# Graph network on one core: edge sums earlier, and the tail's first loads beside the drain

## The chip, the cores and the metric

The kernel runs on one core of one Trainium2 chip, written out by hand for each engine: TensorE (PE), VectorE (DVE), ScalarE (ACT), GpSimd (POOL) and SyncE (SP). The metric is the device time of one execution in microseconds; the median of several runs is quoted, and the profile is of one execution of its own.

## The reference, cut to what matters

```python
h = relu(layernorm(x))                            # 6250 nodes, 256 features
q = (h @ Wq + bq) * 32 ** -0.5;  k = h @ Wk + bk;  v = h @ Wv + bv
s = sum over each head's 32 features of q[src] * k[dst]     # 100000 edges, 8 heads
p = exp(s - max of s over the edges of one src)
att = segment_sum(p / segment_sum(p) * v[dst], src)
x = x + att @ Wo + bo
h = relu(layernorm(x))
aggr = segment_sum(edge_attr, dst)                # 100000 x 256, sorted by dst
u = relu(concat([h, aggr]) @ W1 + b1)
x = x + relu(u @ W2 + b2) @ W3 + b3
```

All of it is float32.

## The kernel before

**Stages.** The edges are first sorted by src on DVE while PE, ACT and SP project q, k and v for 49 tiles of 128 nodes. Then come the *batches*: 214 of them, numbered 2 to 215 (`VB` = 2, `NBT` = 216), each of 512 sorted edge slots. Four batches are a *group* (`SG` = 4). Last comes the *tail*: for each of 49 tiles of nodes the output projection, the layernorm and the three layers of the perceptron.

**One batch.** POOL gathers 512 rows of k and v with four indirect loads (`gather`, L791) into a ring of ten buffers in `U` (`NKG` = 10). PE spreads the query rows over the slots (`group_expand`, L1438). DVE multiplies them with k (L2202), reduces (L2209), once a group runs the chain of segment maxima (`group_chain`, L2217 to L2250), and weights v (`group_weighted`, L2256 and L2258). ACT takes the exponentials. PE adds the weighted rows up per node (`group_weighted`, four matmul calls a batch, eight records at L1452); ACT copies a finished group out (L1088), and SP writes it to `g_log` (L635).

**Order.** Each engine has a function `grouped_rounds`, a loop over rounds `b` from 2 to a few past 215. In round b DVE scores batch b and weights batch b - 5 (`LG` = 5), PE spreads batch b + 2 and adds up batch b - 6, POOL runs ahead as far as free buffers and PE's spreads let it. Extra work is hung on round numbers. After the last round DVE sets `T_ZC`, ACT raises `act_over`, SP waits until every row of `g_log` is written and raises `sp_over`.

**Edge sums.** `aggr` is made beside all this: 98 chunks of 1024 edges, eight *sums* each, a sum being 128 edges against a one-hot matrix (`agg_sum`, L1266, two records). The one-hots are ACT's (L947, L949), ACT issues the loads of 512 KB (L507), SP writes the chunks to `ag_dram`. `agg_by_batch` says how many sums are through after round b: 112 before round 2, all 784 after round 191. From `AE` = 192 hang the steps that need them all: `far_rows` (round 196), masks (195, 199, 203), places, the table of rows `rowi` (209), and the *border sums*: POOL loads one row per chunk after its last gather (`border_sums`), DVE adds `F2` in round 217 (`G2_AT`), POOL stores them back.

**Start of the tail.** SP then loads the sums of tiles 0 to 8 into `pa` (`load_sums`, L666), PE makes the two biases' rows (L1210), turns `pa` with 18 transposes (`turn_sums`, L1564), which ACT copies to `aT` (L1134), and multiplies them by half of W1 into banks that are kept (`sums_by_w1`, L1571). ACT copies the biases to `brep` (L1141). SP loads x per tile (`ld`, L701), POOL the rows of `g_log` by `rowi` (`tiles_in`, L807); six tiles have buffers (`NL` = 6). All these buffers lie in `U`, over the ring. DVE adds the biases to six tiles (`bias_rows`, L2370), then goes tile by tile: `norm_rows` (L2360), `x1_stats` (L2383), and so on. PE's tail loop is `turn_h2` (L1588), `turn_rows` (L1596), `wo_mm` (L1612), then the perceptron (L1629 to L1650).

```python
            with e.Else():
                grouped_rounds()
                e.wait_ge(act_over, 1)
                e.wait_ge(tv.s, T_ZC)
...
            e.wait_ge(s_pa, 16)
            for g, half in ((1, 0), (1, 1), (2, 0), (2, 1), (0, 0)):
                turn_sums(g, half)
```

Of the kernel before, what the change touches and what calls it, by code (L numbers as in the profile page):

```python
# [12 lines left out]
P = 128  # L13
# [40 lines left out]
def gnn_kernel(nc, x, src, dst, ea, Wq, bq, Wk, bk, Wv, bv, Wo, bo, W1, b1, W2, b2, W3, b3, out):  # L54
# [30 lines left out]
    with ExitStack() as st:  # L85
# [171 lines left out]
        MTo = [VG.take(P) for _ in range(2)]  # L257
        fG = base[:, 0:NGR]
# [73 lines left out]
        pa = EBO[:, 0:NPT * D].rearrange("p (t d) -> p t d", d=D)  # L332
        ot = [W.take(RW) for _ in range(NL)]
        xt = [W.take(D) for _ in range(NL)]
        at = [W.take(D) for _ in range(NL)]
# [3 lines left out]
        aT = [W.take(2, 512) for _ in range(3)]  # L339
# [10 lines left out]
        brep = W.take(2, D)  # L350
# [46 lines left out]
        row_mm = sem("row_mm")  # L397
# [30 lines left out]
        def agg_by_batch(b):  # L428

            chunks = NCH - C0  # L430
            m = 0
            while (m + 1) * AE // chunks <= b:
                m += 1
            at, rounds = m * AE // chunks, (m + 1) * AE // chunks - m * AE // chunks
            return AGG0 + 8 * m + -(-8 * (b - at + 1) // rounds) if m < chunks else AGG_STEPS
# [43 lines left out]
        AE = NBT - SG - 20  # L479
# [6 lines left out]
        TURNED = {1: (3, 5), 2: (6, 7), 0: (3,)}  # L486
# [36 lines left out]
        def sync_program(e):  # L523
# [150 lines left out]
            with e.If(more_):  # L674
# [10 lines left out]
                e.sem_inc(sp_over, 1)  # L685
            with e.Else():
                grouped_rounds()
                e.sem_inc(sp_over, 1)
                load_sums()

            def ld(w):
                if w >= NT:
                    return
                i, n = w % NL, rows(w)
                if w == 0:
# [3 lines left out]
                if w >= NL:  # L699
                    e.wait_ge(w_x1, w - NL + 1)  # L700
# [7 lines left out]
            for w in range(3):  # L708
                ld(w)
# [12 lines left out]
        def pool_program(e):  # L722
# [93 lines left out]
            def border_sums():  # L816
                e.wait_ge(row_mm, 3)
                e.wait_ge(all_done, 1)
                assert pl.on(e.memset(G2, 0.0)) == G2Z
                e.wait_ge(pl.s, G2Z)  # L820
                rows_in(G2, ag_dram, NP, ixi[:, 2:3]).then_inc(s_g2, 16)

            def border_sums_back():
                e.wait_ge(tv.s, T_G2)
                rows_out(ag_dram, NP, ixi[:, 2:3], G2).then_inc(s_g2, 16)

            def tiles_in(log, n):
                for w in range(NT):
# [5 lines left out]
            with e.If(more_):  # L834
                for b in range(VB + len(early), NBT):
                    gather(b, NKV)
                border_sums()
# [3 lines left out]
                border_sums_back()  # L841
# [12 lines left out]
                tiles_in(o_log, NB * P)  # L854
# [1614 lines left out]
```

## Time and profile before

| | |
|---|---|
| median of 3 runs | 1730.67 us (1730.32 to 1735.76) |
| the profiled execution's own time | 1730.11 us |
| its span, first to last instruction | 1728.3 us |
| busy share of the span | DVE 88%, PE 86%, POOL 55%, ACT 51% |
| batches | 362 to 1458 us |
| tail | 1458 to 1728 us |

Times inside the span count from its first instruction. A group's time is read between two starts of L2202, four batches apart. PE's records of one matmul overlap, as their ends are modelled; its pace is read from start to start.

### The profile page before, as it was taken

How to read it: one execution, taken by the hardware profiler on the slowest of the kernel's cores; microseconds unless marked ns; L12 is line 12 of the kernel's file. 1: busy time of each engine (PE TensorE's matmuls, PEld its weight loads, DVE VectorE, ACT ScalarE, POOL GpSimd, SP SyncE). 2: the span in 40 equal slices, each digit the busy share in tenths (PEclk: the TensorE clock that was granted, in tenths of full speed). 3: DMA queues.
4: the chain of work that ended last, by engine and by line, in shares of the span. 5: the costliest groups of instructions: out<-in, count | busy, mean ns of one | idle time of the engine just before them, and what ended most of it. 6: DMA issues, size and time to landing. Idle time of an engine off the chain costs nothing.

```text
span 1728.3 us, 25001 instructions
## 1 busy us (share of the span) xinstructions
PE 1486.6 (86%) x6926; PEld 1073.2 (62%) x6926; DVE 1523.7 (88%) x2994; ACT 881.0 (51%) x2624; POOL 950.1 (55%) x1002
## 2 busy tenths in 40 slices
PE   4699998868988899888898888888988765899998
PEld 4545556646766667667766676666766544666664
DVE  9998897879999999999999999999999995766663
ACT  4744445746556556666656555565652000544442
POOL 7000103867777777777777777777777772321200
PEclk9699999979999889999999999988999887999999
DMA  9032325879999999999999999999998772333321
GB/s 235 2 110 101 110 92 201 281 236 339 343 311 323 315 329 323 321 322 332 321 337 326 323 333 326 324 315 332 317 321 263 216 210 96 102 112 110 111 73 37
DMA packets 189586, 411.76 MB, mean 238 GB/s; under 512 B 41449, under 2 KB 101296, under 8 KB 189438
## 3 DMA queue, kind: packets, MB, share of 16 engines
q0 software_dynamic: 71088, 231.68, 40.1%
q1 hardware_dynamic: 91958, 90.12, 16.2%
q10 hardware_dynamic: 26392, 88.26, 14.3%
q8 instruction: 60, 0.98, 0.2%
q14 instruction: 88, 0.72, 0.1%
HBM read 363.56 MB, written 46.35 MB: 237 GB/s over the span
## 4 chain that ended last, share of the span: by engine, by line
DVE 42%; PE 40%; issue 10%; DMA 4%; ACT 3%; POOL 0%; SPq 0%; DVEq 0%; ACTq 0%; POOLq 0%
DVE V L2202 10%; DVE V L2209 9%; PE bank L1452 6%; PE bank L1266 5%; PE bank L1629 4%; DVE V L2258 4%; PE bank L1236 3%; PE bank L1650 2%; PE bank L1638 2%; PE bank L1237 2%; DVE V L1697 2%; PE bank L1612 2%; DVE V L2246 2%; PE bank_pair L1438 2%; DVE V L2232 2%
## 5 line engine op out<-in xcount | busy, mean ns | idle before, releaser
L791 POOL DMA_INDIRECT U<-kv_rows,dstb x856 | 814.7, 952 | 277.5 <-issue 247.1
L1452 PE MATMUL bank<-V 128*128 128x264 f32 x1712 | 475.0, 419 | 5.4 <-DVE V L2258 5.4
L1452 PEld LDWEIGHTS bank<-V 128*128 128x128 f32 x1712 | 349.0, 207 | 101.2 <-issue 31.7
L1266 PE MATMUL bank<-EBO 128*128 128x256 f32 x1568 | 379.4, 384 | 17.0 <-DMA EBO<-in_edge_attr_dram 11.5
L1266 PEld LDWEIGHTS bank<-EBO 128*128 128x128 f32 x1568 | 296.8, 192 | 65.8 <-DMA EBO<-in_edge_attr_dram 15.7
L949 ACT ACTIVATE EBO<-EBO,ones 128x128 f32<-128x128 f32 x728 | 292.4, 402 | 23.6
L947 ACT ACTIVATE EBO<-iota,dA 128x128 f32<-128x128 f32 x728 | 285.8, 393 | 0.3 <-issue 0.2
L1438 PE MATMUL bank_pair<-V 128*128 128x256 f32 x428 | 151.8, 440 | 142.3 <-DVE V L2202 139.5
L2209 DVE TENSOR_REDUCE V<-V 128x32 f32<-128x1024 f32 x214 | 259.8, 1214 | 3.8
L2202 DVE TENSOR_TENSOR V<-U,bank_pair 128x1024 f32<-128x1024 f32 x214 | 259.5, 1213 | 4.1 <-DMA U<-kv_rows,dstb 2.5
L2258 DVE TENSOR_TENSOR V<-U,bank 128x1024 f32<-128x1024 f32 x214 | 259.4, 1212 | 0.8 <-ACT bank L1075 0.8
L1438 PEld LDWEIGHTS bank_pair<-V 128*128 128x128 f32 x428 | 74.3, 206 | 166.1 <-DVE V L2202 159.9
L807 POOL DMA_INDIRECT U<-g_log,rs x49 | 48.9, 999 | 157.8 <-DVE U L2360 142.6
L1075 ACT ACTIVATE bank<-V 128x128 f32<-128x128 f32 x54 | 15.0, 277 | 207.3 <-DVE V L2250 206.8
L770 POOL TENSOR_SCALAR EBO<-iota,dA 128x128 f32<-128x128 f32 x56 | 49.1, 894 | 97.8 <-PE bank L1266 97.8
L1752 DVE TENSOR_TENSOR U<-U 128x512 f32<-128x512 f32 x130 | 90.2, 694 | 4.5
L1753 DVE TENSOR_TENSOR U<-U 128x512 f32<-128x512 f32 x130 | 88.9, 684 | 0.0
L754 POOL MEMSET padneg<- 128x512 f32 x1 | 0.5, 528 | 147.1 <-DVE dA L1779 147.1
L1629 PE MATMUL bank<-U,W_s 128*128 128x512 f32 (+1 forms) x192 | 81.2, 566 | 0.0
L2383 DVE TENSOR_TENSOR U<-U,bank 128x256 f32<-128x256 f32 x49 | 20.5, 419 | 63.4 <-PE bank L1612 63.4
L1088 ACT COPY V<-bank 128x264 f32<-128x264 f32 x28 | 10.6, 379 | 121.8 <-PE bank L1452 121.8
L2256 DVE TENSOR_SCALAR V<-iota,lid 128x128 f32<-128x128 f32 x214 | 70.6, 330 | 1.8 <-PE bank L1452 1.8
(279 smaller groups left out, 2037.3 us busy)
## 6 DMA issues: line engine op xcount, KB each, us to landing
EBO<-in_edge_attr_dram ACTq DMA_DIRECT2D x163, 512.0 KB, 6.6
EBO<-in_edge_attr_dram SPq DMA_DIRECT2D x31, 512.0 KB, 4.7
U<-kv_rows,dstb POOLq DMA_INDIRECT x856, 5.2
kv_rows<-U SPq DMA_DIRECT2D x49, 256.0 KB, 2.0
ag_rows<-R SPq DMA_DIRECT2D x98, 128.0 KB
V<-q_rows SPq DMA_DIRECT2D x54, 128.0 KB, 6.0
q_rows<-U SPq DMA_DIRECT2D x49, 128.0 KB, 1.7
U<-in_x_dram SPq DMA_DIRECT2D x8, 768.0 KB, 9.8
```

The lines of the kernel that those rows point to most:

```text
L791: e.indirect_dma_start(out=kvb[:, b % n, j, :], out_offset=None, in_=kv_dram[:, :], in_offset=bass.IndirectOffsetOnAxis(ap=dstb[:, k:k + 1 ...
L947: a = ab.on(e.activation(oh2[c % 2][:, j, :], iota[:, :], ACT.Abs, bias=dA[:, k:k + 1], scale=-1.0))
L949: e.activation(oh2[c % 2][:, j, :], oh2[c % 2][:, j, :], ACT.Relu, bias=ones[:, 0:1], scale=-1.0).then_inc(a_oha, 1)
L1266: m = e.matmul(agg_bank(c, grouped)[:, 0:D], oh2[i][0:n, j, :], eb[h % NEB][0:n, j % 4, :], start=j == 0, stop=j == 7)
L1438: e.matmul(bank[b % 2][:, 0:D], ohTg[g % 2][:, b % SG, :], qg[g % NQG], start=True, stop=True).then_inc(b_qe, 1)
L1452: t = e.matmul(o[:, 0:RW], ohog[b % NPV], PVg[b % NPV][:, j, :, :].rearrange("p h d -> p (h d)"), start=first and j == 0, stop=y == SG - 1 ...
L1629: t = e.matmul((bank[KEPT[g, f]] if kept else mlp_bank(g, f))[:, 0:n], W1_s[:, (k + 2) % 4, f * P:(f + 1) * P], v[:, 0:n], start=k == 0, s ...
L1752: dv.on(e.tensor_tensor(vb[:, :, 0, :], va[:, :, 0, :], va[:, :, 1, :], ALU.min))
L1753: dv.on(e.tensor_tensor(vb[:, :, 1, :], va[:, :, 0, :], va[:, :, 1, :], ALU.max))
L2202: e.tensor_tensor(Tg, kvb[:, b % NKG, :, 0:D], qv, ALU.mult).then_inc(b_mult, 1)
L2209: e.tensor_reduce(Sg_[:, c0:c0 + 4, :], Tg.rearrange("p j (h d) -> p j h d", d=DH), AX.X, ALU.add).then_inc(b_red, 1)
L2258: e.tensor_tensor(PVg[i][:, :, :, 0:DH], kvb[:, b % NKG, :, D:2 * D].rearrange("p j (h d) -> p j h d", d=DH), pw[g % 2][:, y * 4:y * 4 + 4 ...
```

## The change

Edge sums go at four per round from round 2 and end in round 169; `AE` is 180, and all that hangs on it comes twelve rounds sooner. The border sums are loaded before gather 196 into a tile of their own (`G2g`), added in round 193 and stored before gather 204; `load_sums` is issued in SP's round 206. The buffers of the tail are laid out anew in `U`: x, rows and biases of the first six tiles where batches 206 and 207 were, `aT` and others where 208 and 209 were. So SP loads six x tiles in round 214 and POOL six tiles of rows after its last gather, both once batch 207 is weighted (`ROOM`); each waits for no more row groups than it can need (`groups_to`). PE's bias product is in round 200, ACT's copy in 214. PE turns the sums in rounds 215 to 219 into banks 5 and 6, ACT copies a round later. `sums_by_w1` moves into the tail's steps 2, 3 and 4, and the bias step of the first six tiles into the tail's loop.

```diff
         def agg_by_batch(b):
-            chunks = NCH - C0
...
-            return AGG0 + 8 * m + -(-8 * (b - at + 1) // rounds) if m < chunks else AGG_STEPS
+            return min(AGG0 + 4 * (b - VB + 1), AGG_STEPS)
...
-        AE = NBT - SG - 20
+        AE = NBT - SG - 32
...
+        G2_IN, G2_ADD, G2_OUT = AE + 16, AE + 13, AE + 24
+        PA_AT, BR_AT, BREP_AT, X_AT = AE + 26, AE + 20, NBT - 2, NBT - 2
+        ROOM = NBT - NKG + 2
+        turns_at = {NBT - 1 + i: v for i, v in enumerate(((1, 0), (1, 1), (2, 0), (2, 1), (0, 0)))}
+        TURNED = {1: (5, 6), 2: (5, 6), 0: (5,)}
+
+        def groups_to(w):
+
+            return min(8 * (w + 1) + 1, NGR)
...
+            def first_x():
+                for w in range(NL):
+                    e.dma_start(xt[w], x[w * P:w * P + P, :]).then_inc(s_xa[w], 16)
...
+                    if b == PA_AT:
+                        load_sums()
+                    if b == X_AT:
+                        e.wait_ge(b_pv, ROOM)
+                        first_x()
...
+            def first_tiles():
+                e.wait_ge(rowi_ready, 1)
+                e.wait_ge(b_pv, ROOM)
+                for w in range(NL):
+                    for i in range(NR):
+                        e.wait_ge(s_o[i], 16 * ((groups_to(w) + NR - 1 - i) // NR))
+                    rows_in(ot[w], g_log, groups_to(w) * P, rowi[:, w:w + 1]).then_inc(s_ot[w], 16)
...
                 for b in range(VB + len(early), NBT):
+                    if b == G2_IN:
+                        border_sums(G2g)
+                    elif b == G2_OUT:
+                        border_sums_back(G2g)
                     gather(b, NKG)
-                border_sums()
-                border_sums_back()
+                first_tiles()
                 e.wait_ge(sp_over, 1)
-                e.wait_ge(tv.s, T_ZC)
-                tiles_in(g_log, NGR * P)
+                tiles_in(g_log, NGR * P, NL)
...
+                    if b == BREP_AT:
+                        e.wait_ge(b_pv, ROOM)
+                        bias_spread()
+                    elif b - 1 in turns_at:
+                        e.wait_ge(b_pv, ROOM + 2)
+                        turned_sums(*turns_at[b - 1])
...
+                    if b == BR_AT:
+                        e.wait_ge(rowi_ready, 1)
+                        bias_sums()
+                    elif b in turns_at:
+                        e.wait_ge(g_oh, spread(NGR - 1, 1))
+                        turn_sums(*turns_at[b])
...
             with e.Else():
                 grouped_rounds()
-                e.wait_ge(act_over, 1)
                 e.wait_ge(tv.s, T_ZC)
...
                 if w:
                     e.wait_ge(w_hT2, w)
                 else:
-                    e.wait_ge(pt_ev, 2 * NPG - 1)
+                    e.wait_ge(act_over, 1)
...
+                if 2 <= w < 2 + len(KEPT):
+                    sums_by_w1(*list(KEPT)[w - 2])
...
-            for w in range(NL):
-                bias_rows(w)
...
-                if NL <= w < NT:
+                if w < NT:
                     bias_rows(w)
```

How the instructions stand on an engine is shown at two places. The first is PE at the end of the batches. Before (L1452 adds up a batch, L1451 the row that two groups share, L1210 is the bias product, L1564 the turning, L1571 W1, L1596 a tile's rows):

```order
L1451 MATMUL bank<-R,cont 1x264
L1452 MATMUL bank<-V 128x264 x16
L1451 MATMUL bank<-V,cont 1x264
L1452 MATMUL bank<-V 128x264
L1550 UNCONDITIONAL_BRANCH
L1210 MATMUL bank<-b,ones 128x512
L1564 MATMUL bank<-ident,EBO 128x128 x18
L1571 MATMUL bank<-U,W_s 128x512 x4
L1571 MATMUL bank_pair<-U,W_s 128x512 x2
L1596 MATMUL bank_pair<-ident,U 128x128 x4
L1612 MATMUL bank<-Wo_s,U 128x256 x2
```

Now the same steps are L1486, L1485, L1511 (turning), L1635, L1651 and L1518 (W1), from after batch 211:

```order
L1511 MATMUL bank<-ident,EBO 128x128 x4
L1486 MATMUL bank<-V 128x264 x4
L1511 MATMUL bank<-ident,EBO 128x128 x4
L1486 MATMUL bank<-V 128x264 x4
L1511 MATMUL bank<-ident,EBO 128x128 x2
L1486 MATMUL bank<-V 128x264 x7
L1485 MATMUL bank<-V,cont 1x264
L1486 MATMUL bank<-V 128x264
L1616 UNCONDITIONAL_BRANCH
L1635 MATMUL bank_pair<-ident,U 128x128 x4
L1651 MATMUL bank<-Wo_s,U 128x256 x2
L1518 MATMUL bank<-U,W_s 128x512 x2
```

Ten of the eighteen transposes stand among the last four batches, nothing stands between the last batch and the first tile, and W1 comes after a projection.

The second is POOL from batch 6 on. Before (L791 gathers, L819 clears, L807 loads rows by index, L812 stores them):

```order
L791 DMA U<-kv_rows,dstb 128x512 x840
L819 MEMSET EBO 128x256
L807 DMA EBO<-ag_rows,Wqkv 128x256
L812 DMA ag_rows<-EBO,Wqkv 6272x256
L807 DMA U<-g_log,rs 128x264 x49
```

Now (L808, L835, L824 and L829 are the same steps):

```order
L808 DMA U<-kv_rows,dstb 128x512 x760
L835 MEMSET V 128x256
L824 DMA V<-ag_rows,Wqkv 128x256
L808 DMA U<-kv_rows,dstb 128x512 x32
L829 DMA ag_rows<-V,Wqkv 6272x256
L808 DMA U<-kv_rows,dstb 128x512 x48
L824 DMA U<-g_log,rs 128x264 x49
```

The border sums stand among the gathers, eighty indirect loads before the end, and the store forty-eight before it.

## Rows read from the trace of the kernel before

**Rows 1.** The page: busy time and share of the span by engine.

```profile
PE 1486.6 (86%) x6926; PEld 1073.2 (62%) x6926; DVE 1523.7 (88%) x2994; ACT 881.0 (51%) x2624; POOL 950.1 (55%) x1002
```

**Rows 2.** Stretches: length; busy PE, PEld, DVE, ACT, POOL; PE clock, DMA share, GB/s.

```profile
449.21:469.29 20.08, 19.94 (x96) 16.16 (x95) 19.52 (x37) 16.72 (x51) 15.19 (x16) 1.00 0.96 347
...
833.03:853.24 20.21, 15.88 (x60) 11.81 (x59) 19.65 (x39) 8.75 (x27) 15.22 (x17) 0.83 0.92 310
853.24:873.29 20.05, 20.05 (x103) 16.16 (x101) 19.49 (x37) 15.76 (x49) 14.84 (x17) 1.00 0.97 346
...
388.80:475.00 86.20, 76.49 (x342) 59.95 (x340) 82.61 (x162) 54.26 (x166) 65.17 (x70) 0.94 0.95 341
```

**Rows 3.** DVE's waits, 400 to 1320 us: total us, times, longest.

```profile
DVE V L2202 <- DMA U<-kv_rows,dstb: 1.2, 2, 1.0
```

**Rows 4.** POOL's timeline: start, us, what, idle time before it.

```profile
824.92 0.95 POOL L791 DMA_INDIRECT U<-kv_rows,dstb  x1 [0.30 <-PE bank_pair L1438]
826.17 0.95 POOL L791 DMA_INDIRECT U<-kv_rows,dstb  x1 [0.30 <-issue]
```

**Rows 5.** Landing of the gathers (L791), 1000 to 1200 us, then 1400 to 1430.

```profile
DMA to landing us min/median/max: 3.5/5.3/7.1
...
DMA to landing us min/median/max: 3.5/3.7/4.5
```

**Rows 6.** POOL's timeline after its last gather.

```profile
1428.42 0.33 POOL L819 MEMSET EBO<- 128x256 f32 x1
1429.60 1.03 POOL L807 DMA_INDIRECT EBO<-ag_rows,Wqkv  x1 [0.85 <-POOL EBO L819]
```

**Rows 7.** PE's timeline at the end of the batches.

```profile
1445.84 2.00 PE L1452 MATMUL bank<-V 128*128 128x264 f32 x6 [3.75 <-DVE V L2258]
...
1448.74 8.16 PE L1452 MATMUL bank<-V 128*128 128x264 f32 x32
...
1457.37 0.71 PE L1452 MATMUL bank<-V 128*128 128x264 f32 x2
1458.85 0.39 PE L1210 MATMUL bank<-b,ones 3*128 3x512 bf16 x1 [0.77 <-ACTq L1129]
```

**Rows 8.** Busy time by stretch: PE's clock (PEclk) around the hand-over, and the tail.

```profile
1446.00:1450.00 4.00, 4.00 (x11) 2.11 (x12) 2.77 (x5) 0.00 (x0) 1.02 (x1) 0.61 0.07 25
...
1450.00:1454.00 4.00, 4.00 (x18) 3.36 (x18) 2.89 (x5) 0.80 (x3) 0.00 (x0) 0.96 0.11 38
...
1466.00:1470.00 4.00, 3.65 (x17) 3.65 (x18) 0.00 (x0) 1.76 (x3) 2.00 (x2) 0.50 1.01 338
...
1510.00:1690.00 180.00, 180.00 (x735) 119.72 (x734) 113.92 (x435) 83.30 (x220) 30.26 (x31) 1.00 0.32 98
```

**Rows 9.** The timeline of the hand-over and the first tiles.

```profile
1460.38 0.40 SPq L666 DMA_DIRECT2D EBO<-ag_rows  x1
...
1466.35 4.10 PE L1564 MATMUL bank<-ident,EBO 128*128 128x128 f32 x18 [7.11 <-DMA EBO<-ag_rows]
...
1470.79 3.68 PE L1571 MATMUL bank<-U,W_s 128*128 128x512 f32 x8 [0.34 <-ACT U L1134]
...
1471.51 2.10 DVE L2370 TENSOR_TENSOR U<-U 128x256 f32<-128x256 f32 x6 [17.94 <-ACT U L1141]
...
1476.02 0.38 PE L1596 MATMUL bank_pair<-ident,U 128*128 128x128 f32 x2
...
1480.87 0.44 PE L1588 MATMUL bank<-ident,U 128*128 128x128 f32 x2 [0.94 <-ACT U L1147]
...
1481.46 1.07 PE L1612 MATMUL bank<-Wo_s,U 128*128 128x256 f32 x4
...
1483.48 0.41 DVE L2383 TENSOR_TENSOR U<-U,bank 128x256 f32<-128x256 f32 x1
...
1486.08 0.41 DVE L2383 TENSOR_TENSOR U<-U,bank 128x256 f32<-128x256 f32 x1
...
1489.01 0.41 DVE L2383 TENSOR_TENSOR U<-U,bank 128x256 f32<-128x256 f32 x1
```

More of the change, by code:

```diff
@@ L257, in gnn_kernel @@
         MTo = [VG.take(P) for _ in range(2)]
+        G2g = VG.take(D)
         fG = base[:, 0:NGR]
@@ L332, in gnn_kernel @@
         pa = EBO[:, 0:NPT * D].rearrange("p (t d) -> p t d", d=D)
+        FREE0 = (NBT - NKG) % NKG
+        W.at = FREE0 * 8 * D
+        xt = [W.take(D) for _ in range(NL)]
         ot = [W.take(RW) for _ in range(NL)]
-        xt = [W.take(D) for _ in range(NL)]
-        at = [W.take(D) for _ in range(NL)]
+        brep = W.take(2, D)
+        assert W.at <= (FREE0 + 2) * 8 * D
+        aT = [W.take(2, 512) for _ in range(3)]
         att = [W.take(D) for _ in range(2)]
@@ L338, in gnn_kernel @@
         cT = [W.take(2, P) for _ in range(2)]
-        aT = [W.take(2, 512) for _ in range(3)]
+        assert FREE0 + 4 == NKG and W.at <= NKG * 8 * D
+        W.at = 0
+        at = [W.take(D) for _ in range(NL)]
         x1 = [W.take(D) for _ in range(NX1)]
@@ L814, in rows_out, with border_sums, border_sums_back, tiles_in @@
                     in_=tile, in_offset=None, bounds_check=n - 1, oob_is_err=False)
-            def border_sums():
-                e.wait_ge(row_mm, 3)
+            def border_sums(tile):
                 e.wait_ge(all_done, 1)
-                assert pl.on(e.memset(G2, 0.0)) == G2Z
+                assert pl.on(e.memset(tile, 0.0)) == G2Z
                 e.wait_ge(pl.s, G2Z)
-                rows_in(G2, ag_dram, NP, ixi[:, 2:3]).then_inc(s_g2, 16)
-            def border_sums_back():
+                rows_in(tile, ag_dram, NP, ixi[:, 2:3]).then_inc(s_g2, 16)
+            def border_sums_back(tile):
                 e.wait_ge(tv.s, T_G2)
-                rows_out(ag_dram, NP, ixi[:, 2:3], G2).then_inc(s_g2, 16)
-            def tiles_in(log, n):
-                for w in range(NT):
+                rows_out(ag_dram, NP, ixi[:, 2:3], tile).then_inc(s_g2, 16)
+            def first_tiles():
[5 more added lines that the diff above has]
+                    rows_in(ot[w], g_log, groups_to(w) * P, rowi[:, w:w + 1]).then_inc(s_ot[w], 16)
+            def tiles_in(log, n, first):
+                for w in range(first, NT):
                     if w >= NL:
@@ L1122, in scalar_program @@
                 e.activation(dlT[:, :, 1, :], dlT[:, :, 1, :], ACT.Exp).then_inc(d_exp, 1)
+                bias_spread()
+                for g, half in turns_at.values():
+                    turned_sums(g, half)
             ab.n = n
@@ L1462, in group_turns, with bias_sums, turn_sums, sums_by_w1 @@
                             ident[0:NH, 0:NH]).then_inc(span_out, 1)
+            def bias_sums():
+                bias_mm(bank[6][:, :], 3 * D, 5 * D, True).then_inc(w_br, 1)
+            def turn_sums(g, half):
+                if (g, half) == (1, 0):
+                    e.wait_ge(s_pa, 16)
+                elif (g, half) == (1, 1):
+                    e.wait_ge(w_brep, 1)
+                else:
+                    e.wait_ge(pt_ev, 2 * g + half - 3 if g else 3)
+                n = 2 if g else 1
+                for z in range(2):
+                    for i in range(n):
+                        t = e.transpose(bank[TURNED[g][half]][:, (n * z + i) * P:(n * z + i + 1) * P],
+                                        pa[:, tiles(g)[2 * half + i], z * P:(z + 1) * P], ident[:, :])
+                t.then_inc(pt_tr, 1)
+            def sums_by_w1(g, f):
+                e.wait_ge(pt_ev, 5)
+                for k in range(2):
+                    e.matmul(bank[KEPT[g, f]][:, :], W1_s[:, 2 + k, f * P:(f + 1) * P], aT[g][:, k, :], start=k == 0, stop=False)
             def group_places(p):
```

78 lines of the change are left out of this document (27 added, 51 removed).

## The prediction

> **What bounds the kernel now.** I read the page first, then the busy time of stretches cut at groups of four batches, then the instruction timelines of POOL, DVE and PE, and last the hand-over from the batches to the tail. The page has DVE and PE at 88% and 86% of the span [rows 1]; shares don't say which one sets the end, so the stages are read apart.
>
> In the batches DVE does. A group of four batches takes 20.05 to 20.21 us, and DVE is busy for 19.5 to 19.65 of them, in a group where PE is full as in one where it idles for four [rows 2]. The product of scores (L2202) waits for a gather only twice between 400 and 1320 us, 1.2 us together [rows 3]. Two resources stand close behind. POOL issues its gathers back to back, 1.25 us from one to the next [rows 4]: 16 make 20.0 us a group, so it has almost nothing left. The fourth gather of batch 96 starts at 826.17; the batch's scores start at 833.03, where the stretch of the group is cut, 6.9 us later; a landing takes 5.3 us in the median and 7.1 at most [rows 2, 4, 5]. The reader is to see that the batches can't become faster by moving edge sums, but could become slower.
>
> In the tail PE does: from 1510 to 1690 it is busy for 180.0 of 180 us [rows 8]. Whatever moves PE's start in the tail moves the end by as much, less what is added to PE's work after that start.
>
> Between the two lies a hole. PE's last matmul of the batches ends at 1457.37 + 0.71 = 1458.08 [rows 7]. Then the sums of the first nine tiles are fetched at 1460.38, PE turns them from 1466.35, multiplies them by W1 from 1470.79, and turns the first row tile at 1476.02. DVE starts on the biases at 1471.51, after 17.94 us of idleness, so it had left the batches at 1453.6 [rows 9]. So 1476.02 - 1458.08 = 17.9 us pass between PE's last batch and its first tile.
>
> **The change part by part.**
>
> *Edge sums at four per round.* 672 of them were spread over rounds 2 to 191 and now fill rounds 2 to 169, 42 groups: 16 in every group, where before it was 12, 14 or 16. Their total work is the same on PE, ACT and DMA. PE at its fullest pair of groups (30 sums) still idles for 20.21 - 15.88 = 4.3 us [rows 2]; two sums more are four matmuls, 1.0 us at the 0.255 us of the wider ones in the drain (8.16 / 32) [rows 7]. ACT is busy for 24.5 of those 40.3 us. DMA moved 328 GB/s over that pair; the two extra sums bring 0.26 MB and a little output, so about 335 GB/s. A stretch of 86 us held 341 GB/s, and a group inside it, at 347, took 20.08 us [rows 2]. I take 0 for the loop. Below, a gain is possible: the first round had twelve sums, now four; I give it no term. Above stand the rivals.
>
> The Trainium skill (DMA: Bandwidth & Descriptors, Specifications) puts the HBM limit of one core at about 358 GB/s. By it the denser groups fit as well, and the trace's fullest group, 346, lies under it.
>
> *Masks, places, the table of rows, border sums.* All shift by twelve rounds with the same DVE and PE work: 0. POOL gets the memset, a wait and an indirect load (1429.60 + 1.03 - 1428.42 = 2.2 us) before gather 196, and the store back, about 1.3 us, before gather 204, where both stood behind its last gather [rows 6]; the 1.3 is one issue, 1.03 us, and the gap of 0.30 after it [rows 4, 6]. Behind these 3.5 us stand only gathers; by then no edge tiles are loaded and a landing takes 3.7 us instead of 5.3 [rows 5], so that 1.6 us of them is paid by landings alone, and the masks, each of which holds DVE but not POOL, have by then given POOL more than the rest. I take 0, and 3.5 as the other end. DVE adds the border sums in round 193, before POOL's load in *its* order, but POOL stands three rounds ahead.
>
> *The fetch of the nine tiles' sums* (1.18 MB) moves from 1460 to SP's round 206. It took 6 us to land (1460.38 to 1466.35) [rows 9] and PE asks for it in round 215, nine rounds of 5 us later: 0. What queues behind it on SP are row writes with groups to spare.
>
> *x, biases, rows of tiles 0 to 5.* SP issues six loads and POOL six indirect loads as soon as batch 207 has been weighted, some 20 us before the tail; the buffers of batches 206 and 207 are free then. PE's bias product and ACT's copy lie in rounds 200 and 214. DVE can begin tile 0 right after its last batch: 18 us of idleness go, and PE becomes what is late.
>
> *The turning of the sums* (18 transposes and five copies) moves before the end of PE's batches. PE idles for 3.75 us before batch 211, which hides the first eight. From there on it is full [rows 7], so the last ten are on the path. At a granted clock of 0.50, the level of 1.2 GHz, 18 took 4.10 us [rows 8, 9], 0.23 each; at the end of the batches the clock is 0.96 [rows 8], close to 2.4 GHz, so half of it: 1.1 us (ends: 0, and 2.3 at the low clock). ACT's copies wait for no more than PE has in front of it. Leaving the branch and meeting DVE's flag I put at 0.4 us: before, 0.77 passed from 1458.08 to the bias product at 1458.85, ACT's copy included [rows 7]. So PE starts the tail at 1458.1 + 1.1 + 0.4 = 1459.6 instead of 1476.0: **-16.4 us**.
>
> *The sums by W1* (12 matmuls; the first eight take 3.68 us with the pipeline's end, so 0.43 each, 5.2 us) [rows 9] now follow the output projections of tiles 0, 1 and 2. The ends are 0 and 5.2. Before, DVE paced these tiles: 2.60 us apart (1483.48 to 1486.08) without the bias step, 2.93 with it (to 1489.01) [rows 9]. Now the bias step is in each of them, and PE has 0.6 us of transposes (1480.87 to 1481.46) and 1.1 of projection of its own, the first two of these tiles without the 0.35 of L1588, so 1.4 on average, plus 1.7: 3.1 us. Three intervals grow by 0.5: **+1.5 us**. The later ones were 2.93 already.
>
> *The clock.* In 1446 to 1450 PE's granted clock was 0.61 after 3.75 us of idleness, and batch 211, begun at 1445.84, was not through at 1448.74, while the later ones take 2.0 us each (8 matmuls of 32 in 8.16) [rows 7, 8]. With transposes in that hole it may stay high: up to 1.7 us gained, none taken. The Trainium skill (TensorE: Matmul & The Clock Gate, Part 1) says that an idle array falls back to half clock and activity releases it; by that this gain should come in part, and the rows agree about the fall.
>
> The sum: 1730.1 (the profiled execution's own time) - 16.4 + 1.5 = 1715.2. The median of the runs lies 0.6 above that execution, so 1715.8; I say 1716.
>
> **The rivals.**
>
> *Gathers a little late.* With 16 sums in every group, PE spreads queries later, which holds POOL, and edge tiles press on the landings. If one wait of 0.3 us comes in each of 42 groups, minus what already hides, say in half: 21 x 0.3 = 6, which gives 1722. For it: POOL has no slack. Against: groups of 16 sums took 20.1 us like all others, and PE idles once per pair, which resets its lag.
>
> *Gathers late in every group, slower than before.* The place is the fourth gather before each chain round. Its landing may take 6.9 us. If the edge tiles bring it to 7.4 on average, DVE loses 0.5 us a group; since DVE's delay also delays the query spread that lets POOL go on, the lead doesn't come back: 42 x 0.5 = 21 us, 1737. It decides from a landing of 7.4 us in the median; the trace has 5.3. The Trainium skill (DMA: Bandwidth & Descriptors, Queues, rings and completion order) says that each DMA engine takes turns between the queues it has work for, packet by packet; by it more edge traffic does lengthen gathers. Against: 341 GB/s for 86 us without such waits.
>
> *What is done early waits inside the batches.* PE's turning in round 215 has batches 210 to 215 behind it in order, and waits for the fetched sums, these for POOL's store, this for DVE's sum. If that chain ends late, all of it stands before the last batches instead of behind them, and the 16.4 us are lost: 1732, no change. It needs 45 us of lateness, and no row shows such a wait.
>
> **How the numbers follow.** What a measurement here can tell from no change is 0.3%, 5.2 us. The forecast has 0.80, the small lateness 0.10 (also faster by more than 5.2), the lateness in every group 0.06, the early work that waits 0.04. Faster 0.90, same 0.04, slower 0.06. The range: down to 1712.5, with the W1 products wholly hidden (-1.5) and the clock kept (-1.7); up to 1724, with them unhidden (+3.7) and the turns at half clock (+1.2) or POOL's 3.5 us, and past the small lateness at 1722.
>
> **What would show it.** Groups in the batches should still take 20.05 to 20.2 us, with DVE over 19.4 busy. DVE should start tile 0 within 2 us of its last weighted batch, and PE's first row transposes should stand 1.5 us after the last batch's end. The first projected tiles (x1) should be some 3 us apart. Wrong would be: waits for gathers at L2202 of more than 5 us in sum; a group over 20.5 us; PE idle for over 2 us between batch and tile.

## The result, and the profile after

The changed kernel takes 1711.98 us (median of 4 runs, 1710.05 to 1713.76), the kernel before 1732.22 (4 runs, 1730.32 to 1735.76): ratio 0.9875, 95% interval 0.9858 to 0.9892, so 20.2 us are gained. The forecast was 1716.0 with a range of 1712.5 to 1724: the direction and most of the gain are right, and the time lies 0.5 us below the range.

The profiled execution took 1713.76 us, its span is 1711.9. Busy time and share of the span by engine, page of the changed kernel:

```profile
PE 1479.0 (86%) x6926; PEld 1067.2 (62%) x6926; DVE 1522.8 (89%) x2994; ACT 882.5 (52%) x2624; POOL 950.9 (56%) x1002
```

As in [rows 1], it says nothing of where the time went. Busy time by stretch, changed kernel (columns as in [rows 2]): three groups of batches, four stretches of the hand-over, the tail.

```profile
450.30:470.40 20.10, 18.34 (x87) 14.76 (x86) 19.54 (x37) 15.43 (x47) 15.22 (x17) 1.00 0.95 340
833.50:853.60 20.10, 16.98 (x74) 12.88 (x73) 19.54 (x38) 10.59 (x33) 15.23 (x17) 0.92 0.94 329
853.60:873.70 20.10, 20.03 (x101) 16.20 (x99) 19.54 (x36) 16.48 (x50) 15.23 (x17) 1.00 0.97 346
1446.00:1450.00 4.00, 3.28 (x16) 2.21 (x17) 3.78 (x7) 0.81 (x3) 0.00 (x0) 1.00 0.00 0
1450.00:1454.00 4.00, 4.00 (x22) 3.40 (x21) 2.92 (x7) 1.49 (x4) 0.00 (x0) 1.00 0.09 34
1454.00:1458.00 4.00, 4.00 (x19) 2.81 (x18) 1.97 (x8) 0.37 (x1) 0.00 (x0) 1.00 0.00 0
1458.00:1462.00 4.00, 3.15 (x14) 2.00 (x14) 1.80 (x6) 2.41 (x4) 0.56 (x1) 1.00 0.10 36
1490.00:1670.00 180.00, 180.00 (x735) 119.75 (x734) 115.39 (x440) 83.73 (x222) 31.11 (x32) 1.00 0.32 101
```

The groups take 20.1 us as before, DVE is busy for 19.5 of them, and DMA moves 329 to 346 GB/s [rows 2]. The gathers (L808, 1000 to 1200 us) land a little later in the median than in [rows 5]:

```profile
DMA to landing us min/median/max: 3.7/5.6/6.7
```

DVE waits for nothing between 400 and 1320 us. PE's granted clock, 0.61 in the stretch of batch 211 and 0.50 in the turning [rows 8], is now 1.00 through the hand-over.

Starts differ by chance before the first scores (362.5 us into the span before, 366.9 after, 363.4 to 366.6 in six later executions with an equally fast loop, in code that is the same). So the stages are read from the first scores (L2202, now L2243) to the scores of batch 215, and from there to the end:

| us | before | after | |
|---|---|---|---|
| scores of batch 8, from the first | 25.36 | 22.91 | -2.45 |
| batch 12 | 46.50 | 43.06 | -3.44 |
| batch 170 | 845.37 | 841.58 | -3.79 |
| batch 215 | 1073.73 | 1070.14 | -3.59 |
| last weighted product ends, from the scores of batch 215 | 21.88 | 21.40 | -0.48 |
| PE's first row tile | 39.82 | 21.24 | -18.58 |
| x1 of tile 0 | 42.07 | 23.79 | -18.28 |
| x1 of tile 3 | 49.88 | 32.63 | -17.25 |
| end (start of the last instruction) | 292.04 | 274.80 | -17.24 |

The spans, 1728.3 and 1711.9, differ by 16.4 alone, since this execution reached its batches 4.5 us later. The whole gain is 3.6 in the batches, nearly all of it in the first rounds, and 17.2 in the hand-over.

PE's timeline of the hand-over, changed kernel (start, us, what, idle time before it and its releaser):

```profile
1446.72 1.60 PE L1486 MATMUL bank<-V 128*128 128x264 f32 x6 [3.32 <-DVE V L2299]
...
1453.78 0.38 PE L1511 MATMUL bank<-ident,EBO 128*128 128x128 f32 x2
...
1457.75 0.71 PE L1486 MATMUL bank<-V 128*128 128x264 f32 x2
1458.31 0.38 PE L1635 MATMUL bank_pair<-ident,U 128*128 128x128 f32 x2
1459.54 0.41 PE L1635 MATMUL bank_pair<-ident,U 128*128 128x128 f32 x2 [0.85 <-ACT U L1197]
...
1462.37 0.38 PE L1635 MATMUL bank_pair<-ident,U 128*128 128x128 f32 x2
...
1465.39 0.38 PE L1635 MATMUL bank_pair<-ident,U 128*128 128x128 f32 x2
```

The hole of 17.9 us is gone: the first row tile starts with no gap behind the last product, and batch 211 took 1.60 us for the rows that took 2.00 [rows 7]. DVE's timeline there:

```profile
1453.23 0.06 DVE L2388 MEMSET over<- 1x1 f32 x1
1453.44 0.17 DVE L2397 TENSOR_SCALAR U<-U 128x8 f32<-128x8 f32 x1
...
1460.86 0.42 DVE L2424 TENSOR_TENSOR U<-U,bank 128x256 f32<-128x256 f32 x1 [1.30 <-PE bank L1651]
...
1463.80 0.41 DVE L2424 TENSOR_TENSOR U<-U,bank 128x256 f32<-128x256 f32 x1
...
1466.74 0.41 DVE L2424 TENSOR_TENSOR U<-U,bank 128x256 f32<-128x256 f32 x1
```

DVE begins tile 0 at 1453.44, 0.2 us after its last batch, and x1 comes every 2.94 us. In the first round, 12 sums (24 matmuls, 6.13 us from 366.88) stood before PE's next spreads; now 4 do. The waits of PE for edge tiles, 351 to 400 us of the kernel before, and 355 to 405 of the changed one:

```profile
PE bank L1266 <- DMA EBO<-in_edge_attr_dram: 7.5, 4, 3.7
```

```profile
PE bank L1300 <- DMA EBO<-in_edge_attr_dram: 2.9, 1, 2.9
```

PE stood still for edge tiles 7.5 us before and 2.9 after; behind it waited the spread, and behind that POOL's gathers (9.3 us before, 5.6 after).

### The profile page after: what moved, and what is told of

It reads as the page before. It is cut to its first block, busy times and chain, and to the rows that moved or that the text cites. A ratio compares the mean times of both kernels' runs of the same rounds, so it can differ in the third digit from the quotient of the medians.

```text
span 1711.9 us, 25023 instructions
## 1 busy us (share of the span) xinstructions
PE 1479.0 (86%) x6926; PEld 1067.2 (62%) x6926; DVE 1522.8 (89%) x2994; ACT 882.5 (52%) x2624; POOL 950.9 (56%) x1002
## 3 DMA queue, kind: packets, MB, share of 16 engines
q1 hardware_dynamic: 91958, 90.12, 16.4%
## 4 chain that ended last, share of the span: by engine, by line
PE 48%; DVE 41%; issue 8%; DMA 1%; POOL 1%; ACT 0%; SPq 0%; DVEq 0%; ACTq 0%
PE bank L1486 10%; DVE V L2243 9%; PE bank L1300 8%; DVE V L2250 8%; PE bank L1668 4%; DVE V L2299 4%; PE bank_pair L1472 3%; PE bank L1270 3%; PE bank L1689 3%; PE bank L1271 2%; PE bank L1677 2%; DVE V L1738 2%; PE bank L1651 2%; DVE V L2287 2%; DVE V L2273 2%
## 5 line engine op out<-in xcount | busy, mean ns | idle before, releaser
L808 POOL DMA_INDIRECT U<-kv_rows,dstb x856 | 815.6, 953 | 271.6 <-issue 246.4
L1486 PE MATMUL bank<-V 128*128 128x264 f32 x1712 | 469.7, 416 | 4.2 <-DVE V L2299 4.2
L1486 PEld LDWEIGHTS bank<-V 128*128 128x128 f32 x1712 | 344.2, 204 | 96.3 <-issue 30.9
L1300 PE MATMUL bank<-EBO 128*128 128x256 f32 x1568 | 379.4, 387 | 14.9 <-DMA EBO<-in_edge_attr_dram 7.9
L2243 DVE TENSOR_TENSOR V<-U,bank_pair 128x1024 f32<-128x1024 f32 x214 | 259.4, 1212 | 1.6 <-PE bank_pair L1472 1.1
L824 POOL DMA_INDIRECT U<-g_log,rs x49 | 48.7, 995 | 158.3 <-DVE U L2401 133.3
L963 ACT COPY U<-bank 128x512 f32<-128x512 f32 x49 | 28.7, 586 | 72.5 <-PE bank L1271 72.5
```

Of the source, the lines that this page charges most:

```text
L808: e.indirect_dma_start(out=kvb[:, b % n, j, :], out_offset=None, in_=kv_dram[:, :], in_offset=bass.IndirectOffsetOnAxis(ap=dstb[:, k:k + 1 ...
L1300: m = e.matmul(agg_bank(c, grouped)[:, 0:D], oh2[i][0:n, j, :], eb[h % NEB][0:n, j % 4, :], start=j == 0, stop=j == 7)
L1486: t = e.matmul(o[:, 0:RW], ohog[b % NPV], PVg[b % NPV][:, j, :, :].rearrange("p h d -> p (h d)"), start=first and j == 0, stop=y == SG - 1 ...
L2243: e.tensor_tensor(Tg, kvb[:, b % NKG, :, 0:D], qv, ALU.mult).then_inc(b_mult, 1)
```

## The experiments

Three theories of the difference from the forecast were put to the test: (A) the batches' 3.6 us are the first round's sums; (B) the hand-over is bound by one chain after another, each worth what the change moved; (C) the +1.5 for W1 is really DVE's bias step. There were 18 runs of eleven kernels in five sessions (the recorded expectations say "call") on three chips; a session is a set of kernels measured together on one chip.

### The loop was not as fast in every session

In two sessions the kernel before took 1734 us, in two others 1941, and one of the chips met both. In the fifth (the runs whose labels end in "alone", and hole_filled) it has no time of its own on record; the kernels there ran at the slow pace. Nearly all of the difference lies in the batches: 24 us a group instead of 20. A stretch of the batches, changed kernel of the first measurement, then the run sums_alone:

```profile
400.00:1300.00 900.00, 799.92 (x3642) 623.60 (x3641) 875.01 (x1597) 545.88 (x1662) 679.61 (x715) 0.95 0.94 327
```

```profile
400.00:1300.00 900.00, 743.29 (x3086) 570.91 (x3087) 726.21 (x1320) 493.32 (x1502) 558.05 (x591) 0.88 0.83 280
```

DMA moves 280 GB/s instead of 327, and every engine is less busy, DVE by 149 of 900 us: it no longer sets the pace. DVE's scores wait for gathers 61 us in all in sums_alone (1.2 before [rows 3]), so the loop is bound by what it loads. The tail takes the same time as ever where the clock holds (274.8 us from the last scores on with the changed hand-over). What made the loads late isn't in these traces. A slower transfer of the packets alone doesn't account for it: the gathers' packets kept the DMA engines busy for 59.4% of 1000 to 1200 us for 41.5 MB in the changed kernel and for 50.2% for 33.8 MB in sums_alone, 4% more per MB, while the whole rate fell by 14%. The Trainium skill (HBM Reference, Specifications (TRN2)) says that the two cores of a pair share one memory's bandwidth; work on the other core is one possible cause, and no run here shows it. Below, sessions of this kind are called *loaded*, and from them mainly the tail is read.

### The parts of the hand-over

All four are the changed kernel with one part undone (measured together, one execution each; kernel before 1734.39).

**turn_late** (1715.44 us):

```diff
-                    elif b in turns_at:
-                        turn_sums(*turns_at[b])
...
                 grouped_rounds()
+                for g, half in turns_at.values():
+                    turn_sums(g, half)
```

> The changed kernel with one part undone: the sixteen transposes of the edge sums and their copies stand behind TensorE's last batch and ScalarE's last weights, in a row, instead of one among the last batches each. Everything is read from the first scores of batch 215, since chips differ in the loop before. If the theory of the prediction is right (the turns cost nothing where they stand and keep TensorE's clock up, and in a row they stand between the last sum and the tail), TensorE's first row tile starts 4 to 5 us after its last batch instead of 0.2 us, the last weighted product of the drain ends up to 1 us later (batch 211 meets the lower clock again), and x1 of tile 3 and the end of the kernel come 2.5 to 3.5 us later than in the changed kernel (part of the wait falls beside VectorE's own start of the tail). The rival: VectorE sets the start of the tail, and neither x1 of tile 3 nor the end moves by more than 0.5 us.

ACT's copies move in the same way. First row tile 2.85 us behind the last product instead of 4 to 5, x1 of tile 3 and the end 3.25 and 3.24 us later. The last product ended at 21.88, as before the change: the 1.1 us of turns in front of it are gone, and the clock fell again (0.77 and 0.66 where it was 1.00). So 1.6 of the 3.24 are the clock. Whether the turns kept it up or it would have fallen anyway, one execution doesn't tell.

**w1_first** (1717.10 us):

```diff
+            for g, f in KEPT:
+                sums_by_w1(g, f)
             for w in range(4 * NG + 5):
...
-                if 2 <= w < 2 + len(KEPT):
-                    sums_by_w1(*list(KEPT)[w - 2])
```

> The changed kernel with the twelve products by W1 of the first three groups ahead of the tail's first row tile, instead of four each beside row tiles 2 to 4. Theory of the prediction: TensorE sets the start of the tail and the twelve products are 5.2 us of it, so its first row tile starts 5.2 us later and x1 of tile 3 and the end 4 to 5 us later (1 us less than the 5.2, since VectorE's bias steps no longer lie behind TensorE). The rival: VectorE sets the start (its bias steps and x1), and the end moves by under 1.5 us.

First row tile 6.73 us later, end 6.44; 1.58 of both are the clock, which fell here in code that is the same (last product at 22.98). Without it 5.15 and 4.86, as expected: keeping the products out of the way is worth 4.9 us. The run tells one thing more. No product stands among its first tiles, and still x1 comes every 2.94 us:

```profile
1464.21 0.42 DVE L2424 TENSOR_TENSOR U<-U,bank 128x256 f32<-128x256 f32 x1 [1.00 <-PE bank L1651]
1467.16 0.41 DVE L2424 TENSOR_TENSOR U<-U,bank 128x256 f32<-128x256 f32 x1
1470.10 0.41 DVE L2424 TENSOR_TENSOR U<-U,bank 128x256 f32<-128x256 f32 x1
```

PE idles for 0.93 and 1.28 us between these tiles, and DVE goes from one to the next without waiting for PE. So DVE, with the bias step in each tile, sets 2.94.

**x_late** (1719.79 us):

```diff
-                    if b == X_AT:
-                        first_x()
...
                 e.sem_inc(sp_over, 1)
+                first_x()
```

> The changed kernel with the loads of x for the first tiles issued after SP's last row write instead of six batches before the end. What the part is worth: if x is waited for, TensorE's first row tile stays where it was, x1 of tile 0 comes 2 to 4 us later (the load's landing of some 2.5 to 4 us against the 2.4 us between the last product and x1), and the end moves with it or by a part of it. The rival: the first row tile and the scores' turn hide it, and x1 of tile 0 and the end move by under 0.5 us.

The first row tile stays (21.23), but x1 of tile 0 is 5.48 us later and the end 6.81, over the range expected. DVE's timeline of x_late says why:

```profile
1453.11 0.42 DVE L2399 TENSOR_TENSOR U<-U 128x256 f32<-128x256 f32 x1
1461.88 0.42 DVE L2409 TENSOR_TENSOR U<-U 128x256 f32<-128x256 f32 x1 [8.35 <-DMA U<-in_x_dram]
```

Not x1 but the bias step (L2409) waits for x, and on DVE it stands in front of the norm of tile 1; so PE's second row tile comes 5.23 us after PE ran out of work. Its clock is down to 0.50 by then:

```profile
1463.00:1466.00 3.00, 2.86 (x7) 2.17 (x8) 1.88 (x7) 1.66 (x2) 1.84 (x2) 0.50 0.55 170
```

The end moves by 1.33 us more than x1 of tile 0 does; PE at half its clock in these tiles is the likely reason, and no run takes it away.

**rows_late** (1722.43 us):

```diff
-                first_tiles()
                 e.wait_ge(sp_over, 1)
+                first_tiles()
```

> The changed kernel with the gathers of the tail's first row tiles issued behind SP's last row write and its semaphore, as before the change, and all else as changed. If the hand-over was bound by this chain (write, semaphore, rows in, land), TensorE's first row tile starts 6.5 to 7.5 us later than in the changed kernel, and the end moves by the same. The rival: the rows land in time for most of it and under 3 us are lost, the rest of the gain then being the sums' turning alone.

First row tile 9.04 us later, end 10.43; 1.58 is the clock in the drain again, so 7.46, inside the range expected, and 8.85, over it. The difference has the look of x_late's: PE idled for 7.30 us, and its clock was 0.50 and 0.56 in the six us behind. The chain of write, flag, six loads is the longest of the four. B holds: to undo one part costs 3.2, 4.9, 6.8 and 8.9 us, of which 1.6 (turn_late) and some 1.3 and 1.4 (the last two) go with PE's lower clock behind the longer hole; the chains overlap and don't add up to the 17.2.

### The first round's sums

Three kernels: **sums_alone** is the kernel before with the new `agg_by_batch` and nothing else; **first_four** is the kernel before with its own spread cut to four sums in the first round and four more per round until it has caught up; **first_twelve** is the changed kernel with twelve sums in the first round.

```diff
 first_four
-            return AGG0 + 8 * m + -(-8 * (b - at + 1) // rounds) if m < chunks else AGG_STEPS
+            n = AGG0 + 8 * m + -(-8 * (b - at + 1) // rounds) if m < chunks else AGG_STEPS
+            return min(n, AGG0 + 4 * (b - VB + 1))
 first_twelve
-            return min(AGG0 + 4 * (b - VB + 1), AGG_STEPS)
+            return min(AGG0 + 8 + 4 * (b - VB + 1), AGG_STEPS)
```

> The kernel before with one line changed: edge sums at four per round from round 2, all else (masks, border sums, tail) where it was. Theory A (the unforecast 4 us come from the first round, which has 4 sums instead of 12): the scores of batch 12 start 43.1 us after the first scores instead of 46.5, later groups take 20.05 to 20.2 us, and the time falls by 3 to 4 us. Rival B (they come from another part, or from chance before the batches): batch 12 at 46.5 us after the first scores, time unchanged. Rival C (16 sums in every group press on the gathers): groups over 20.3 us, time up by several us.

> The kernel before with its old spread of edge sums, but never more than four per round, so only the first rounds are lighter (the first twelve become four, and eight are made up in rounds 5 to 15). Theory A: the same 3 to 4 us as with the whole new spread, batch 12 at 43.1 us after the first scores. Rival B: nothing. If the density of the later groups costs or gives something, this kernel and the one with the whole new spread differ by it; A says they are equal within 1 us.

> The changed kernel with twelve sums in round 2 again, then four per round. Theory A: it gives 3 to 4 us back, about 1715.5, with the scores of batch 12 at 46.5 us after the first scores, and gather 8 some 3.5 us later. Rival B: it stays at the changed kernel's time, 1712.

The session was loaded (before 1941.7): 1937.85, 1934.63 and 1935.68 us, ratios 0.9985 (0.9973 to 0.9998), 0.9966 (0.9952 to 0.9979) and 0.9965 (0.9948 to 0.9981). Batch 12 came at 49.65, 52.17 and 57.43, where the changed kernel itself, in the next session, has 48.89: the stages can't be told apart. A second session was loaded too:

> The kernel before with one thing changed: at most four sums in the first round and four more per round from there until its own spread has caught up. If the first round's sums are what the prediction priced at 0, batch 12 starts 43 us after the first scores instead of 46.5, and the time is 3 to 4 us under the kernel before. The rival: no change within 1 us.

> The changed kernel with eight more sums in the first round (twelve, as before the change). If the 3.8 us that the batches gained are the first round's sums, then batch 12 starts 46.5 us after the first scores instead of 43.0, the loop is 3 to 4 us longer than in the changed kernel up to batch 170, and the time is 3 to 4 us over it. The rival: the gain belongs to the even spread of the sums over the groups, and both are unchanged within 0.5 us.

1934.51 (0.9962, 0.9947 to 0.9977) and 1933.10 (0.9964, 0.9949 to 0.9979). The times do say one thing: first_four is faster than the kernel before in both sessions, by some 7 us, clear of "nothing". Twelve sums cost the changed kernel 2.5 us there, within the noise. Loaded too were the single executions first_twelve_alone and first_four_alone (1936.48, 1936.41). In the last session the loop was as fast as in the first measurement:

> The changed kernel with eight more sums in the first round, once more, since the loop of first_twelve_alone was bound by loads (24 us a group) and five executions of the changed kernel's own first rounds, in the undisturbed loop, agree within 0.1 us (batch 12 at 43.0). If the groups take 20.06 us here: batch 12 at 46.5 and batch 170 at 845 if the first round's sums are the cause, 43.0 and 841.6 if the even spread is. If the groups take 24 us, nothing is told apart.

> The kernel before with at most four sums in the first round, once more. If the groups take 20.06 us here: batch 12 at 43.0 and batch 170 at 841 to 842 if the first round's sums are the cause, 46.5 and 845.4 if not. If the groups take 24 us, nothing is told apart.

| from the first scores, us | before | after | first_twelve_last | first_four_last |
|---|---|---|---|---|
| batch 8 | 25.36 | 22.91 | 24.70 | 22.91 |
| batch 12 | 46.50 | 43.06 | 47.87 | 42.95 |
| batch 170 | 845.37 | 841.58 | 847.55 | 843.69 |
| batch 215 | 1073.73 | 1070.14 | 1076.23 | 1072.20 |
| time | 1733.84 | | 1717.30 | 1731.98 |

(The last row is of that session, one execution each.) Twelve sums put back cost the changed kernel 4.8 us by batch 12; four in place of twelve give the kernel before 3.55 by batch 12, the whole of what the change gave by then. For the first rounds A holds. PE's waits in first_twelve_last, 364 to 412 us:

```profile
PE bank L1300 <- DMA EBO<-in_edge_attr_dram: 6.0, 5, 3.0
```

That is against 2.9 in the changed kernel, and POOL's gathers waited for PE's spread for 9.8 us instead of 5.6; first_four_last has 2.8 and 5.8, against 7.5 and 9.3 in the kernel before.

At batch 170 both missed their marks: first_twelve_last came at 847.55 where 845 was expected, first_four_last at 843.69 where 841 to 842 was, half way to the rival's 845.4. From batch 12 to 215 first_four_last loses 2.0 us of its 3.55, and first_twelve_last falls 1.3 further behind the changed kernel. Some of this is chance: batch 215 came at 1069.73 to 1071.41 in the five fast executions of the changed loop. So 1.5 of the 3.6 us are shown up to the end of the batches by taking the first round's sums away, and 3.5 up to batch 12 alone; what first_four_last lacks of the changed loop, the even spread above all, is worth 0.8 to 2.5 us in these executions, and not settled.

### W1, the bias step and the clock

**spread_w1**: the changed kernel, bias steps of the first six tiles before tile 1, and the products in pairs.

```diff
+            W1_AT = {1: (1, 0, 0), 2: (1, 0, 1), 3: (1, 1, 0), 4: (1, 1, 1), 7: (2, 0, 0), 8: (2, 0, 1)}
...
-                if 2 <= w < 2 + len(KEPT):
-                    sums_by_w1(*list(KEPT)[w - 2])
+                if w in W1_AT:
+                    sums_by_w1(*W1_AT[w])
...
-                if w < NT:
+                if w == 1:
+                    for v in range(NL):
+                        bias_rows(v)
+                if NL <= w < NT:
                     bias_rows(w)
```

> The changed kernel with two things moved in the tail: the bias step of tiles 2 to 5 is done by DVE while it waits for PE's first transposes, and the six products by W1 are spread, one each over PE's steps 1, 2, 3, 4, 7 and 8 instead of two in each of steps 2, 3 and 4. Theory D (the 1.04 us that the first tiles lost are DVE's bias steps, and the W1 products were hidden): the first projected tiles stand 2.6 to 2.7 us apart instead of 2.94, and 0.5 to 1 us is gained by tile 9, too little for the time to show. Rival E (PE paces them): still 2.9 us apart.

1929.53 us in the loaded session (0.9930, 0.9908 to 0.9953). x1 of tile 3 at 31.59 instead of 32.62 and the end at 273.82 instead of 274.80: x1 every 2.61 us, 1.0 us gained and kept. The run changes two things at once; that w1_first keeps 2.94 without any product says that the bias step is the one that counts. The other runs of it, in the next session with the changed kernel beside it:

> The changed kernel itself, as the measure for the other kernels of this call. If the chip's memory is as in the first measurement (kernel before 1732 us), 1712 us with all in the loop at 20.06 us a group and DVE hardly waiting; if it is as in the call that gave 1941 us for the kernel before, some 1933, with groups of 24 us. TensorE's last weighted product comes 21.4 us after the first scores of batch 215 where the clock holds through batch 211, and 23.0 where it falls to the lower level (both have been seen with the same transposes in the hole).

> A version meant to beat both: the changed kernel with the six pairs of products by W1 spread over the tail's steps 1, 2, 3, 4, 7 and 8, the bias steps of the first six tiles together before tile 1, and sixteen transposes of the identity (their result is not used) in TensorE's idle time before batch 211, to keep its clock. Theory: x1 of tile 3 comes 1.0 us earlier and stays so (31.6 instead of 32.6 us after the scores of batch 215), and the clock holds in every execution, worth 1.6 us in those in which it would have fallen; together 1 to 2.6 us under the changed kernel. The rival: the clock falls just the same in some executions, and only 1.0 us is gained.

1930.61 (0.9941, 0.9924 to 0.9958) and 1927.79 (0.9934, 0.9917 to 0.9951): 2.8 us apart, but the intervals overlap. The clock was not kept: PE ran the idle transposes one batch too early, ahead of batch 210, the hole before batch 211 stayed 3.04 us long, and the clock was 0.61 behind it (last product at 23.02).

> The changed kernel with W1 spread over the tail's steps 1, 2, 3, 4, 7, 8 and the first six bias steps together before tile 1, as a single execution. In the calls with many rounds x1 of tile 3 came 31.6 us after the scores of batch 215 instead of 32.6 and the end as much sooner; the same is expected here, 1.0 us under the changed kernel for the same clock in the drain.

> spread_w1_alone with twenty transposes of the identity (result unused) behind the turning of round 216, so in TensorE's idle time before batch 211 itself; in spread_w1_kept_clock sixteen such stood one batch earlier, ahead of batch 210, and the hole behind them was as long as before (3.0 us) and the clock 0.61 in it. If the fall comes from the hole itself, the granted clock in the 3 us behind it is over 0.95, the weighted products of batch 211 take under 1.7 us and the last one ends 21.4 us after the scores of batch 215. The rival: the clock falls here too (last product at 23.0). The executions of the changed kernel have fallen both ways without it, so one run that keeps the clock is weak evidence and one that falls is strong.

```diff
 hole_filled
                         turn_sums(*turns_at[b])
+                        if b == NBT:
+                            for k in range(20):
+                                e.transpose(bank[0][:, (k % 4) * P:(k % 4 + 1) * P], ident[:, :], ident[:, :])
```

PE's clock in the two stretches around batch 211, first spread_w1_alone, then hole_filled:

```profile
1651.62:1654.62 3.00, 2.35 (x5) 1.85 (x6) 3.00 (x5) 0.36 (x2) 0.00 (x0) 0.50 0.00 0
1654.62:1657.62 3.00, 3.00 (x8) 1.22 (x7) 0.41 (x2) 0.16 (x1) 0.00 (x0) 0.50 0.00 0
```

```profile
1662.99:1665.99 3.00, 2.95 (x26) 2.63 (x24) 2.80 (x10) 0.71 (x3) 0.00 (x0) 1.00 0.00 0
1665.99:1668.99 3.00, 2.36 (x9) 1.44 (x10) 3.00 (x5) 0.35 (x2) 0.00 (x0) 1.00 0.00 0
```

spread_w1_alone (1921.23) met the fall at its worst, 0.50, last product at 24.31 and end at 276.73; 2.9 of that are the clock, which leaves the 273.8 expected. hole_filled (1932.66) kept 1.00, 21.39 and 273.80. Over all executions but hole_filled, the changed order kept the clock in seven (last product at 21.4) and lost it in five (22.98 to 23.02 in four, 24.31 in one). The holes before batch 211 were not equally long: 1.99, 2.33 and 2.51 us in three loaded executions, which all kept it, and 3.04 to 3.32 us in the other nine, of which four kept it and five lost it. The order before, turn_late among it, had 3.58 to 3.75 us, lost it in six (21.70 to 21.89) and kept it in one, first_four_alone (20.28). 21.40 - 20.28 = 1.12 us is what the turns cost at the high clock, by this one execution. That a filled hole always keeps it isn't shown by one run. Whether spread_w1 and hole_filled beat the changed kernel in the fast loop was not run; what is measured is their tail.

### What the loaded sessions show of the change

There the changed kernel gained 10.8 us instead of 20.2, though the hand-over kept its 17.2, or 15.9 where the clock fell, as in changed_again. changed_again took 145.5 us from batch 192 to 215, sums_alone 136.1 (before the change and after it, in the fast loop: 120.3 and 116.8). DVE's waits in that stretch of changed_again:

```profile
DVE V L2243 <- issue: 10.0, 3, 5.0
DVE V L2355 <- DMA V<-ag_rows,Wqkv: 5.2, 1, 5.2
```

L2355 adds the border sums: DVE reaches it in round 193 before POOL's load has landed, and the scores of the group wait (27.6 us for batches 192 to 196). All eight loaded executions of the changed order have this wait, of 1.6 to 6.2 us; the six in the fast loop have none, but the lead there is thin: POOL issues the load 3.2 us before DVE's add in the profiled execution. "POOL stands three rounds ahead" is true where the loop is bound by DVE, and not where it is bound by loads. The rest of what is lost in loaded sessions is open; the 10.0 us in the first line have no releaser in the trace.

## Why the prediction was right or wrong

**The step that failed** is in *Edge sums at four per round*: "the first round had twelve sums, now four; I give it no term." By batch 12 the term is -3.4 us in the two profiled executions and -3.55 with that one thing changed (first_four_last); by batch 215 the change has -3.6 and first_four_last -1.5, so the rest of the loop's gain is not settled. It was mis-sized because steady groups were read, where PE has slack; in the first rounds the twelve sums take PE 6.13 us in one piece, the sums behind them wait for late edge tiles (7.5 us in all, now 2.9), and both stand in front of the spreads on which scores and gathers hang.

**The rest of the batches**: 0, as forecast; groups of 20.06 us, no wait at the scores. Both rivals of late gathers fell in the fast loop: the landing median rose from 5.3 to 5.6 us, under the 6.9 that there are. In the loaded sessions part of it did come about, at the border sums.

**The hand-over**: forecast -16.4, measured -18.58 at the first row tile. The hole was 39.82 - 21.88 = 17.94. The turns on the path cost 1.12 us against 1.1 forecast. The branch and the flag, 0.4 forecast, cost nothing: the first row tile starts 0.16 us before the modelled end of the last product, 0.56 better than forecast. The clock, named as a gain of up to 1.7 and given no term, brought 1.60 in the profiled execution, though in five of twelve executions it fell all the same: that it held in the measured one is luck. 17.94 - 1.12 + 0.16 + 1.60 = 18.58. The rule quoted from the Trainium skill (TensorE: Matmul & The Clock Gate, Part 1) fits in both directions; behind holes of 3.04 to 3.32 us both outcomes stand in the traces.

**W1 in the tail**: forecast +1.5. The whole tail gave back 18.58 - 17.24 = 1.34 us by tile 3, of which 1.0 was got back by spread_w1. The size was right by luck, and the cause wrong: the forecast had PE's products pace these tiles at 3.1 us. x1 came every 2.94 us, DVE's own pace with the bias step (0.34 more than 2.60), and it does so in w1_first without a product among them. The other 0.3 lie before x1 of tile 0, where PE's second transposes wait 0.85 us for ACT's copy.

**The early work that waits inside the batches** (1732) did not come: PE waited for no fetched sum.

Together: -3.6 - 17.2 = -20.8 from the stages of two executions, -20.2 by the medians, -14.9 forecast. The range was cut at 1712.5 by taking two gains; the third, the first round, had been named and left out. (Its upper end doesn't come out of its terms either: 1716 + 3.7 + 3.5 is 1723.2.)

## What to carry to other kernels

Read the first rounds of a loop apart from its steady groups: work that is free there can stand in front of everything in round one, where no engine has run ahead yet. When a chain behind a loop is moved into it, price each link by undoing it alone, and expect the last one to leave a smaller floor, here DVE's bias step. Work moved under the cover of an engine that runs ahead is hidden only as long as that lead holds: check it in a slower loop too. And when two causes give the same size, look for a run that takes only one away.

## What the runs showed of the hardware

- The same program (the changed kernel) moved 327 GB/s in its loop in one session and 282 in another; the kernel before took 1734 and 1941 us, on one and the same chip. The slow loop came with single executions and with many. Only comparisons inside a session hold, and a change can be worth half as much in one of them (10.8 against 20.2 us).
- TensorE's granted clock behind a hole of 3.0 to 3.3 us went both ways, with nearly the same instructions around it: 1.00 in four of nine executions, 0.6 to 0.8 in four and 0.50 in one in the 3 us behind it, which cost 0, 1.6 and 2.9 us on the path. The changed kernel alone did both (after: hole 3.32, clock 1.00; changed_again: 3.21, 0.70).
